# Perceiver block on one core: the end of the kernel with batch 1's attention sum in TensorE's bank and roundings on ScalarE

## The chip, the cores and the metric

The kernel runs on 1 core of one Trainium2 chip. The metric is the device time of one execution in microseconds, as the median of several runs. Engines are TensorE (PE in the profile, its weight loads PEld), VectorE (DVE), ScalarE (ACT), GpSimd (POOL) and SyncE (SP, which issues the DMAs).

## The reference

Two sequences of 256 tokens of 256 features pass through three parts, each added to the running input: a decoder of four layers with cross attention, one windowed attention, and a feed forward part with quantised weights and activations. The change lies in the last two.

```python
x = x + _L0_xattn_ref(_layernorm(x), ctx, ...)
x = x + _L0_attn_ref(_layernorm(x), ...)      # y = xn + msg @ wo.T; layernorm(y) * gamma + beta
x = x + _L0_ffn_ref(_layernorm(x), ...)
def _act_quant(x):
    scale = 127.0 / jnp.clip(jnp.max(jnp.abs(x), axis=-1, keepdims=True), 1e-05)
    xq = jnp.clip(jnp.round(x * scale), -128.0, 127.0) / scale
gate = jax.nn.silu(_bitlinear(x, w_gate)); up = _bitlinear(x, w_up)
return _bitlinear(gate * up, w_down)          # weights -1, 0, 1 times a scale; inner size 1024
```

## The kernel before

The 512 tokens are four tiles of 128 (t = 0 to 3), two for each batch b. `X0` holds the running input, `hs` (rows of the tile `HE`) the normalised tokens, `X` (rows of `XE`) a scratch tile and the outputs. Four fp32 banks `psD` of 512 columns take TensorE's results in turn (`next_bank`); four more, the tile `QD`, take the gate and up products in two pairs `QB[j]`, one for each half j of the 1,024 inner features.

Each engine runs its own list of steps, written out by hand near the end of its block (TensorE L1185 to 1229, ScalarE up to L1823, VectorE L2530 to 2582, GpSimd up to L2809). Steps meet through semaphores alone, so the order of each list decides what queues behind what. On VectorE `done` adds to a semaphore and waits for it, so that a step that reads its predecessor's result starts after it.

The end, for batch 1, goes so. TensorE multiplies the attention's messages `oT` with the output weight (`out_proj`, L539 to 548). VectorE adds the normalised tokens (`window_sum`), takes mean and variance (`layernorm_stats`; GpSimd forms the power -0.5, `ln_rsqrt`), applies gamma (`window_gamma`), adds to `X0` (`window_residual`), and takes mean and variance again. `layernorm_apply(7, 1)` normalises, `round_tokens` finds each token's largest magnitude, scales, and rounds by adding and subtracting the number MAGIC (12582912), which leaves whole numbers in bf16. TensorE transposes these (`rounded_T`, L787) and VectorE copies the transposed tile back (L2141).

Then for each tile t: TensorE forms gate and up products in halves (`quantised_gate_up`, L797); ScalarE applies silu (`quantised_gates`, L1485); VectorE multiplies gate and up (`quantised_hidden`, L2146), finds the maximum and scale of the 1,024 products (`hidden_scales`, four instructions in `quantise_scales` and L2157); ScalarE scales and adds MAGIC (`scale_hidden`, L1490); VectorE subtracts it (`round_hidden`, L2159); TensorE transposes (`hidden_T`, L809); VectorE copies back (`hidden_T`, L2163); TensorE multiplies with the down weight (`quantised_down`, L818); VectorE scales and adds to `X0` (`output`, L2168); SyncE stores the tile (L1307). The down weight is made ternary by ScalarE in two pieces (`ternary(2)`, `ternary(3)`, L1475), and the first down product waits for both:

```python
pe.wait_ge(tern_set, 4)
pe.wait_ge(*emptied(NL, f"gT{t}"))
```

A gate product of tile t waits until VectorE has read the same pair of banks for tile t - 1 (`quad_free(qu_free, 2 * t + j + 1, ...)`).

## Time and profile before

| | |
|---|---|
| median of 3 runs | 574.45 us (574.3 to 574.61) |
| the profiled execution | 574.83 us |
| its span in the profile | 573.09 us (573.1 on the page) |
| granted TensorE clock, mean | 0.997 of full speed |
| TensorE, VectorE, ScalarE, GpSimd busy | 521.0, 349.2, 283.2, 113.4 us |
| end of the last VectorE instruction | 569.96 us |

The span runs from the first to the last recorded instruction or transfer; the execution's own time has 1.74 us around it. Busy shares are averages over the whole span. To see one stage, a view is cut to a stretch of time: which engine has no gaps, and what the others wait for. In a row of the order of time, the first number is the start, the second the time from the first start to the last end of the merged instructions, and the bracket gives the idle time before and what ended it.

### The profile page before, as it was taken

To read this page: it belongs to the slowest core of one execution; us is meant where nothing else is said; L and a number is where in the kernel's file an instruction comes from. 1 tells how busy PE (TensorE), PEld (TensorE's weight loads), DVE (VectorE), ACT (ScalarE), POOL (GpSimd) and SP (SyncE) were. 2 spreads that over 40 slices of the span, in tenths; PEclk is the share of its full clock that TensorE was granted. 3 is DMA by queue.
4 is the path that set the end of the run, shared out by engine and by line. 5 is a ranking of instruction groups with operands and counts; after the bars stand their busy time and mean duration, and the time that the engine had idled before them with its cause. 6 is when DMAs were issued, how large, how long until landed. Compare 5 with 4: busy or idle time off the path is not lost.

```text
span 573.1 us, 15284 instructions
## 1 busy us (share of the span) xinstructions
PE 521.0 (91%) x6586; PEld 405.8 (71%) x6586; DVE 349.2 (61%) x669; ACT 283.2 (49%) x509; POOL 113.4 (20%) x126
## 2 busy tenths in 40 slices
PE   5888898999998999999998989999989989999764
PEld 3566665988777767988676659988667669987523
...
GB/s 303 182 2 2 3 314 18 11 65 1 196 65 3 13 63 3 74 0 1 222 2 39 75 2 1 75 1 101 122 8 24 76 1 2 1 0 2 2 2 42
DMA packets 5515, 30.40 MB, mean 53 GB/s; under 512 B 1217, under 2 KB 2113, under 8 KB 3778
## 3 DMA queue, kind: packets, MB, share of 16 engines
...
## 4 chain that ended last, share of the span: by engine, by line
PE 76%; DVE 13%; ACT 8%; issue 2%; DMA 0%; POOL 0%; DVEq 0%
PE psD L350 16%; PE QD L694 14%; PE psD L707 10%; PE QD L446 7%; PE QD L486 5%; DVE AQ L1918 4%; ACT PTR L1353 4%; PE psD L344 3%; PE psD L506 3%; PE QD L479 3%; PE psD L694 2%; PE psD L527 2%; PE psD L513 2%; PE psD L387 2%; DVE MX L1915 2%
## 5 line engine op out<-in xcount | busy, mean ns | idle before, releaser
L1353 ACT ACTIVATE PTR<-QD 128x2048 f32<-128x2048 f32 x40 | 75.2, 1880 | 52.8 <-PE QD L486 46.1
L1918 DVE TENSOR_REDUCE AQ<-QD 128x8 f32<-128x2048 f32 (+1 forms) x24 | 55.0, 2292 | 29.4 <-PE QD L446 29.3
L694 PE MATMUL QD<-HH,WFH 128*128 128x256 f32 x224 | 69.0, 308 | 0.0
L2607 POOL TENSOR_TENSOR rstd<-ms,mhalf 128x2 f32<-128x2 f32 x26 | 18.3, 705 | 232.6 <-ACT HE L1319 231.5
L694 PE MATMUL QD<-HL,WFH 128*128 128x256 f32 x224 | 63.3, 282 | 0.0
L694 PE MATMUL QD<-HH,WFL 128*128 128x256 f32 x224 | 63.2, 282 | 0.0
L1915 DVE TENSOR_REDUCE MX<-QD 128x16 f32<-128x2048 f32 x16 | 36.7, 2294 | 39.6 <-PE QD L446 39.6
L707 PE MATMUL psD<-WC,HID 128*128 128x256 f32 x256 | 58.5, 381 | 0.0
L2023 DVE TENSOR_TENSOR WFL<-WC,WFH 128x512 fp32r<-128x512 f32 x64 | 44.4, 701 | 18.6 <-ACT WFH L1399 18.1
L350 PE MATMUL psD<-WAB,hT 128*128 128x256 f32 (+1 forms) x152 | 52.8, 485 | 1.0 <-DVE hT L1856 1.0
L2654 POOL TENSOR_SCALAR_AFFINE_SELECT PTR<-PTR 128x1024 f32<-128x1024 f32 (+1 forms) x24 | 34.5, 1440 | 93.0 <-ACT PTR L1353 93.0
L707 PEld LDWEIGHTS psD<-WC,HID 128*128 128x128 f32 x256 | 47.5, 190 | 7.3 <-issue 1.0
L1399 ACT ACTIVATE WFH<-WC 128x512 fp32r<-128x512 f32 x64 | 40.2, 630 | 24.7 <-PE QD L694 24.1
L446 PE MATMUL QD<-AQ 32*128 32x128 f32 (+1 forms) x1024 | 46.5, 312 | 0.0
L694 PEld LDWEIGHTS QD<-HH,WFH 128*128 128x128 f32 x224 | 42.7, 191 | 3.0 <-issue 2.7
L694 PEld LDWEIGHTS QD<-HH,WFL 128*128 128x128 f32 x224 | 42.8, 191 | 1.7 <-issue 1.4
L694 PEld LDWEIGHTS QD<-HL,WFH 128*128 128x128 f32 x224 | 42.7, 191 | 0.0
L446 PEld LDWEIGHTS QD<-AQ 32*128 32x128 f32 x1024 | 35.1, 185 | 7.7 <-issue 5.5
L1319 ACT ACTIVATE HE<-XE 128x257 f32<-128x257 f32 x48 | 19.7, 413 | 38.3 <-DVE XE L1960 38.3
L350 PEld LDWEIGHTS psD<-WAB,hT 128*128 128x128 f32 x152 | 27.7, 194 | 14.7 <-issue 10.6
L350 PE MATMUL psD<-WAB,oT 128*128 128x256 f32 x144 | 35.3, 388 | 3.0 <-ACT oT L1365 3.0
L1361 ACT ACTIVATE QO<-psD 128x512 f32<-128x512 f32 (+1 forms) x40 | 20.5, 513 | 34.3 <-PE psD L513 18.1
...
## 6 DMA issues: line engine op xcount, KB each, us to landing
...
```

What stands on the lines that cost most here:

```text
L350: mm = pe.matmul(bank(l, use)[:, col:col + n], lhs(k), rhs(k), start=(k == 0), stop=(k == KT - 1))
L446: mm = pe.matmul(quad[a][:, at:at + keys], QKT[b][rows(a), s, q * P:(q + 1) * P], QKT[b][rows(a), s, L:L + keys], start=False, stop=True, ...
L486: mm = pe.matmul(quad[a][:, at:at + P], QKT[b][rows(a), s, L + k * P:L + (k + 1) * P], Q2[rows(a), n * P:(n + 1) * P], start=(at == 0), st ...
L694: mm = pe.matmul(S[:, w * L:(w + 1) * L], wp[:, m, :], hp[:, k, :], start=(k == 0 and j == 0), stop=(k == KT - 1 and j == 2))
L707: mm = pe.matmul(bank(l, use)[:, t * D:(t + 1) * D], AT[b][:, f, t * P:(t + 1) * P], Wd[:, f, :], start=(f == 0 and t == 0), stop=(f == FT ...
L1353: nc.scalar.activation(PTR[:, r % 2, :], QD[:, :], ACT.Exp, scale=SCALE if r < SELF_ROUNDS else 1.0).then_inc(t_exp, 1)
L1361: nc.scalar.activation(OA[:, 0:n], bank(l, use)[:, 0:n], ACT.Copy).then_inc(free(l, use), 1)
L1399: nc.scalar.activation(w_high(n), WCt[:, :, f * P:(f + 1) * P], ACT.Copy).then_inc(wh_set, 1)
L1915: v = dve.tensor_reduce(MX[:, :, ss[0] // 2, :].rearrange("p t (r c) -> p r c t", r=SG_H)[:, :, at:at + 2, :], QD[:, :].rearrange("p (r s ...
L1918: v = dve.tensor_reduce(QKR[b][:, t, 0, h, MAXROW].rearrange("p (s r) -> p r s", r=SG_H), QD[:, :].rearrange("p (r s n) -> p r s n", r=4, ...
L2023: dve.tensor_tensor(w_low(n), WCt[:, :, f * P:(f + 1) * P], w_high(n), ALU.subtract).then_inc(wl_set, 1)
L2654: nc.gpsimd.affine_select(T, T, [[0, 16 // (t + 1)], [1, P]], ALU.is_ge, 0.0, base=0, channel_multiplier=-1)\
```

## The change

It has four parts, all in the end of the kernel.

- The sum of batch 1's attention: TensorE first multiplies the normalised tokens with the identity into the bank `mwo1`, then adds the projection to it (`out_proj_on_tokens`). VectorE's addition goes; statistics and gamma read the bank (`window_sum_stats`, `window_sum_gamma`).
- Batch 1's tokens: ScalarE subtracts them from their mean (`centre`), VectorE takes the maximum of that and forms one factor out of the two scales, with its sign turned (`centred_scales`), ScalarE scales and rounds (`scale_tokens`, `unbias_tokens`). The gates and up products no longer wait for a second scale product (`token_sgu` makes both at once).
- The gated tiles 0 to 2 are rounded on ScalarE (`unbias_hidden`). The upper limit of 127 moves into the copies of the transposed tiles. The maximum, clamp and reciprocal become three steps that stand apart in VectorE's list, and the scale for the output is formed by GpSimd (`hidden_sgu`).
- The last gated tile is scaled half on VectorE, half on ScalarE, then rounded on VectorE, transposed and copied in halves of 512.

The diff, with indentation cut, without declarations of semaphores and without the lists of ScalarE and VectorE, whose result the rows below it show:

```diff
+def out_proj_on_tokens(b, source):
+    use = f"mwo{b}"
+    next_bank(NL, use)
+    pe.wait_ge(an_set[b], 1)
+    pe.wait_ge(*free_for(NL, use))
+    for t in range(QT):
+        pe.matmul(bank(NL, use)[:, t * D:(t + 1) * D], ident, hs[:, 2 * b + t, :], start=(t == 0), stop=False,
+                  skip_group_check=True)
+    pe.wait_ge(*emptied(NL, source))
+    for t in range(QT):
+        for k in range(KT):
+            mm = pe.matmul(bank(NL, use)[:, t * D:(t + 1) * D], oT[b][:, k, t * P:(t + 1) * P], Wt[:, 3, k, :],
+                           start=False, stop=(k == KT - 1), skip_group_check=True)
+    mm.then_inc(full(NL, use), 1)
...
+def last_hidden_T(half):
+    use = f"gT{LAST}{half}"
+    next_bank(NL, use)
+    pe.wait_ge(last_set, half + 1)
+    pe.wait_ge(*free_for(NL, use))
+    for n in range(FT // 2):
+        at = half * F // 2 + n * P
+        mm = pe.transpose(bank(NL, use)[:, :].bitcast(BF16)[:, n * P:(n + 1) * P], GQ(LAST)[:, at:at + P], identB[:, :])
+    mm.then_inc(full(NL, use), 1)
 def quantised_down(t):
     next_bank(NL, f"d{t}")
     pe.wait_ge(tern_set, 4)
-    pe.wait_ge(*emptied(NL, f"gT{t}"))
     pe.wait_ge(*free_for(NL, f"d{t}"))
+    if t < LAST:
+        pe.wait_ge(*emptied(NL, f"gT{t}"))
     for f in range(FT):
+        if t == LAST and f % (FT // 2) == 0:
+            pe.wait_ge(*emptied(NL, f"gT{LAST}{f // (FT // 2)}"))
         mm = pe.matmul(bank(NL, f"d{t}")[:, 0:D], GQT(t)[:, f * P:(f + 1) * P],
                        WQ[2][:, f * D:(f + 1) * D], start=(f == 0), stop=(f == FT - 1))
     mm.then_inc(full(NL, f"d{t}"), 1)
     window_pv(1, 1)
-    out_proj(NL, 1, "mwo1", Wt[:, 3, :, :], "pw1")
+    out_proj_on_tokens(1, "pw1")
     rounded_T(0)
     quantised_gate_up(0, 0)
     quantised_gate_up(0, 1)
     rounded_T(1)
     quantised_gate_up(2, 0)
     quantised_gate_up(2, 1)
+    hidden_T(0)
     quantised_gate_up(3, 0)
     quantised_gate_up(3, 1)
-    hidden_T(0)
     hidden_T(1)
     quantised_down(0)
     hidden_T(2)
+    last_hidden_T(0)
+    last_hidden_T(1)
     quantised_down(1)
-    hidden_T(3)
     quantised_down(2)
     quantised_down(3)
...
 def quantised_gates(t, j):
-    act.wait_ge(sgu_set, t // 2 * 2 + 2)
+    act.wait_ge(sgu_set, t // 2 + 1)
     act.wait_ge(qg_full, 2 * t + j + 1)
...
+def scale_last_hidden():
+    act.wait_ge(gq_scale_set, LAST + 1)
+    nc.scalar.activation(GU(LAST)[:, F // 2:F], GU(LAST)[:, F // 2:F], ACT.Copy, scale=am2[:, LAST, 2:3], bias=MAGIC)\
+      .then_inc(last_scaled, 1)
+def centre(b):
+    act.wait_ge(ln_var[b], 4)
+    for t in range(QT):
+        a = nc.scalar.activation(hs[:, 2 * b + t, :], X0[:, 2 * b + t, :], ACT.Identity, scale=-1.0,
+                                 bias=mv[:, 6 + b, t, 0:1])
+    a.then_inc(cen_set, 1)
+def scale_tokens(b):
+    act.wait_ge(tok_scale_set, 1)
+    for t in range(QT):
+        a = nc.scalar.activation(hs[:, 2 * b + t, :], hs[:, 2 * b + t, :], ACT.Copy, scale=am[:, 2 * b + t, 1:2], bias=MAGIC)
+    a.then_inc(tok_scaled, 1)
+def unbias_tokens(b):
+    act.wait_ge(tok_scaled, 1)
+    for t in (2 * b, 2 * b + 1):
+        nc.scalar.activation(xq[:, t, :], hs[:, t, :], ACT.Copy, bias=-MAGIC).then_inc(xq_set[b], 1)
+def unbias_hidden(t):
+    act.wait_ge(gq_scaled, t + 1)
+    nc.scalar.activation(GQ(t), GU(t), ACT.Copy, bias=-MAGIC).then_inc(gq_set, 1)
...
+def window_sum_stats(b):
+    use, n = f"mwo{b}", 4 + b
+    dve.wait_ge(*filled(NL, use))
+    for t in range(QT):
+        v = dve.bn_stats(bst[:, n, t, :], bank(NL, use)[:, t * D:(t + 1) * D])
+    done(v)
+    for t in range(QT):
+        v = dve.bn_aggr(mv[:, n, t, :], bst[:, n, t, :])
+    done(v)
+    dve.tensor_scalar(lve[:, n, :], mv[:, n, :, 1], LN_EPS, None, ALU.add).then_inc(ln_var[b], 1)
+def window_sum_gamma(b):
+    use = f"mwo{b}"
+    for t in range(QT):
+        v = dve.scalar_tensor_tensor(hs[:, 2 * b + t, :], bank(NL, use)[:, t * D:(t + 1) * D], mv[:, 4 + b, t, 0:1],
+                                     vec[:, D:2 * D], ALU.subtract, ALU.mult)
+    v.then_inc(free(NL, use), 1)
+    dve.wait_ge(*emptied(NL, use))
...
-    for w in range(2):
-        dve.tensor_scalar(sgu[:, 2 * b:2 * b + 2, w], am[:, 2 * b:2 * b + 2, 3], mw[:, w:w + 1], None, ALU.mult)\
-           .then_inc(sgu_set, 1)
+    token_sgu(b)
+def token_sgu(b):
+    dve.tensor_tensor(sgu[:, 2 * b:2 * b + 2, 0:2], am[:, 2 * b:2 * b + 2, 3].unsqueeze(2).broadcast_to([P, 2, 2]),
+                      mw[:, 0:2].unsqueeze(1).broadcast_to([P, 2, 2]), ALU.mult).then_inc(sgu_set, 1)
+def centred_scales(b):
+    ts = slice(2 * b, 2 * b + 2)
+    dve.wait_ge(cen_set, 1)
+    done(dve.tensor_reduce(am[:, ts, 0], hs[:, ts, :], AX_X, ALU.max, apply_absolute_value=True))
+    dve.wait_ge(ln_rstd[b], 4)
+    done(dve.tensor_tensor(am[:, ts, 0], am[:, ts, 0], lrs[:, 6 + b, :], ALU.mult))
+    done(dve.tensor_scalar(am[:, ts, 3], am[:, ts, 0], 1e-5, 1.0 / 127.0, ALU.max, ALU.mult))
+    done(dve.reciprocal(am[:, ts, 2], am[:, ts, 3]))
+    dve.scalar_tensor_tensor(am[:, ts, 1], am[:, ts, 2], -1.0, lrs[:, 6 + b, :], ALU.mult, ALU.mult).then_inc(tok_scale_set, 1)
+    token_sgu(b)
 def rounded_T(b):
     dve.wait_ge(*filled(NL, f"fn{b}"))
     dve.tensor_scalar(xqT[b][:, :, :].rearrange("p k n -> p (k n)"), bank(NL, f"fn{b}")[:, :].bitcast(BF16)[:, 0:KT * L],
-                      -128.0, None, ALU.max).then_inc(free(NL, f"fn{b}"), 1)
+                      -128.0, 127.0, ALU.max, ALU.min).then_inc(free(NL, f"fn{b}"), 1)
 def quantised_hidden(t, j):
-    dve.wait_ge(sgu_set, t // 2 * 2 + 2)
+    dve.wait_ge(sgu_set, t // 2 + 1)
     dve.wait_ge(qu_full, 2 * t + j + 1)
     dve.wait_ge(qg_free, 2 * t + j + 1)
     dve.scalar_tensor_tensor(GU(t)[:, j * 512:(j + 1) * 512], QB[j][1],
                              sgu[:, t, 1:2], GR(t)[:, j * 512:(j + 1) * 512], ALU.mult, ALU.mult)\
        .then_inc(qu_free, 1)
-def hidden_scales(t):
+def hidden_max(t):
     dve.wait_ge(qu_free, 2 * t + 2)
-    quantise_scales(t, 1, GU(t).unsqueeze(1), 1)
-    dve.tensor_scalar(sgu[:, t, 2:3], am2[:, t, 3:4], mw[:, 2:3], None, ALU.mult).then_inc(gq_scale_set, 1)
-def round_hidden(t):
-    dve.wait_ge(gq_scaled, t + 1)
-    dve.tensor_scalar(GQ(t), GU(t), MAGIC, 127.0, ALU.subtract, ALU.min).then_inc(gq_set, 1)
+    dve.tensor_reduce(am2[:, t:t + 1, 0], GU(t).unsqueeze(1), AX_X, ALU.max, apply_absolute_value=True).then_inc(gq_max_set, 1)
+def hidden_clamp(t):
+    dve.wait_ge(gq_max_set, t + 1)
+    dve.tensor_scalar(am2[:, t:t + 1, 3], am2[:, t:t + 1, 0], 1e-5, 1.0 / 127.0, ALU.max, ALU.mult).then_inc(gq_step_set, 1)
+def hidden_inverse(t):
+    dve.wait_ge(gq_step_set, t + 1)
+    dve.reciprocal(am2[:, t:t + 1, 2], am2[:, t:t + 1, 3]).then_inc(gq_scale_set, 1)
 def hidden_T(t):
     dve.wait_ge(*filled(NL, f"gT{t}"))
-    dve.tensor_scalar(GQT(t), bank(NL, f"gT{t}")[:, :].bitcast(BF16), -128.0, None, ALU.max)\
+    dve.tensor_scalar(GQT(t), bank(NL, f"gT{t}")[:, :].bitcast(BF16), -128.0, 127.0, ALU.max, ALU.min)\
        .then_inc(free(NL, f"gT{t}"), 1)
+def scale_last_hidden():
+    dve.wait_ge(gq_scale_set, LAST + 1)
+    done(dve.tensor_scalar(GU(LAST)[:, 0:F // 2], GU(LAST)[:, 0:F // 2], am2[:, LAST, 2:3], MAGIC, ALU.mult, ALU.add))
+def round_last_hidden(half):
+    if half:
+        dve.wait_ge(last_scaled, 1)
+    at = slice(half * F // 2, (half + 1) * F // 2)
+    dve.tensor_scalar(GQ(LAST)[:, at], GU(LAST)[:, at], MAGIC, 127.0, ALU.subtract, ALU.min).then_inc(last_set, 1)
+def last_hidden_T(half):
+    use = f"gT{LAST}{half}"
+    dve.wait_ge(*filled(NL, use))
+    at = slice(half * F // 2, (half + 1) * F // 2)
+    dve.tensor_scalar(GQT(LAST)[:, at], bank(NL, use)[:, :].bitcast(BF16)[:, 0:F // 2], -128.0, None, ALU.max)\
+       .then_inc(free(NL, use), 1)
 def output(t):
-    dve.wait_ge(gq_scale_set, t + 1)
+    dve.wait_ge(hidden_sgu_set, t + 1)
     dve.wait_ge(*filled(NL, f"d{t}"))
     dve.scalar_tensor_tensor(X[:, t, :], bank(NL, f"d{t}")[:, 0:D], sgu[:, t, 2:3], X0[:, t, :],
                              ALU.mult, ALU.add).then_inc(free(NL, f"d{t}"), 1)
     layernorm_stats(6, 0, X0)
     layernorm_apply(6, 0, X0, hs, done)
     round_tokens(0)
-    window_sum(1)
-    layernorm_stats(5, 1, X)
+    window_sum_stats(1)
     rounded_T(0)
-    window_gamma(1)
+    window_sum_gamma(1)
     window_residual(1)
     layernorm_stats(7, 1, X0)
...
+def hidden_sgu(t):
+    pool.wait_ge(gq_scale_set, t + 1)
+    nc.gpsimd.tensor_tensor(sgu[:, t, 2:3], am2[:, t, 3:4], mw[:, 2:3], ALU.mult)\
+        .then_inc(hidden_sgu_set, 1)
```

GpSimd's list ends with `hidden_sgu(0)` to `hidden_sgu(3)`.

ScalarE from the first gates to its end. Before (`AQ<-QD,sgu` is a gate step, `AQ<-AQ,am` a scaling, `WC<-WF,negmagic` the ternary weight):

```order
L1488 ACTIVATE AQ<-QD,sgu 128x512 [waits qg_full,sgu_set] x7
L1492 ACTIVATE AQ<-AQ,am 128x1024 [waits gq_scale_set]
L1482 ACTIVATE WC<-WF,negmagic 128x1024 [waits tern_step]
L1492 ACTIVATE AQ<-AQ,am 128x1024 [waits gq_scale_set]
L1488 ACTIVATE AQ<-QD,sgu 128x512 [waits qg_full,sgu_set]
L1492 ACTIVATE AQ<-AQ,am 128x1024 [waits gq_scale_set] x2
```

ScalarE in the changed kernel, from the gates of tile 1's second half (`HID<-AQ` is the rounding of a gated tile):

```order
L1523 ACTIVATE AQ<-QD,sgu 128x512 [waits qg_full,sgu_set]
L1527 ACTIVATE AQ<-AQ,am 128x1024 [waits gq_scale_set]
L1554 ACTIVATE HID<-AQ 128x1024 [waits gq_scaled]
L1523 ACTIVATE AQ<-QD,sgu 128x512 [waits qg_full,sgu_set] x2
L1527 ACTIVATE AQ<-AQ,am 128x1024 [waits gq_scale_set]
L1554 ACTIVATE HID<-AQ 128x1024 [waits gq_scaled]
L1523 ACTIVATE AQ<-QD,sgu 128x512 [waits qg_full,sgu_set] x2
L1517 ACTIVATE WC<-WF,negmagic 128x1024 [waits tern_step]
L1527 ACTIVATE AQ<-AQ,am 128x1024 [waits gq_scale_set]
L1554 ACTIVATE HID<-AQ 128x1024 [waits gq_scaled]
L1531 ACTIVATE AQ<-AQ,am 128x512 [waits gq_scale_set]
```

The gates of tiles 2 and 3 now stand behind scaling and rounding of tiles 0 and 1, and the ternary weight behind the last gates.

VectorE between the two first gated products and tile 2's. Before (`HE` are the tokens, `QO` their rounded copy and its transpose, `am<-AQ` a maximum):

```order
L2150 SCALAR_TENSOR_TENSOR AQ<-QD,sgu,AQ 128x512 [waits qg_free,qu_full,sgu_set] x2
L2056 TENSOR_SCALAR HE<-X,mv,lrs 128x256 [waits ln_rstd1]
L2056 TENSOR_SCALAR HE<-X,mv,lrs 128x256
L2076 TENSOR_REDUCE am<-HE 128x2 [waits v_step]
L2077 TENSOR_SCALAR am<-am 128x2 [waits v_step]
L2078 RECIPROCAL am<-am 128x2 [waits v_step]
L2133 TENSOR_SCALAR HE<-HE,am 128x256 [waits v_step]
L2133 TENSOR_SCALAR HE<-HE,am 128x256
L2136 TENSOR_SCALAR QO<-HE 128x256 [waits v_step]
L2136 TENSOR_SCALAR QO<-HE 128x256
L2138 TENSOR_SCALAR sgu<-am,mw 128x2 x2
L2150 SCALAR_TENSOR_TENSOR AQ<-QD,sgu,AQ 128x512 [waits qg_free,qu_full,sgu_set] x2
```

VectorE in the changed kernel, the same place:

```order
L2251 SCALAR_TENSOR_TENSOR AQ<-QD,sgu,AQ 128x512 [waits qg_free,qu_full,sgu_set] x2
L2234 TENSOR_REDUCE am<-HE 128x2 [waits cen_set]
L2236 TENSOR_TENSOR am<-am,lrs 128x2 [waits ln_rstd1,v_step]
L2237 TENSOR_SCALAR am<-am 128x2 [waits v_step]
L2238 RECIPROCAL am<-am 128x2 [waits v_step]
L2239 SCALAR_TENSOR_TENSOR am<-am,lrs 128x2 [waits v_step]
L2227 TENSOR_TENSOR sgu<-am,mw 128x2x2
L2257 TENSOR_REDUCE am<-AQ 128x1 [waits qu_free]
L2251 SCALAR_TENSOR_TENSOR AQ<-QD,sgu,AQ 128x512 [waits qg_free,qu_full,sgu_set]
L2261 TENSOR_SCALAR am<-am 128x1 [waits gq_max_set]
L2244 TENSOR_SCALAR QO<-psD 128x512 [waits d_full3]
L2265 RECIPROCAL am<-am 128x1 [waits gq_step_set]
```

Six token steps of 256 are gone from the list, and tile 0's maximum stands before the gated products of tile 1.

## Rows read from the trace of the kernel before

**Rows 1.** The page, part 1: busy time, share, instructions.
```profile
PE 521.0 (91%) x6586; PEld 405.8 (71%) x6586; DVE 349.2 (61%) x669; ACT 283.2 (49%) x509; POOL 113.4 (20%) x126
```
**Rows 2.** Busy time by stretch; the last columns are granted clock, DMA share, GB/s.
```profile
505.00:541.27 36.27, 34.00 (x472) 27.59 (x470) 15.69 (x47) 19.93 (x26) 9.65 (x9) 1.00 0.01 2
541.27:569.96 28.69, 16.17 (x104) 8.22 (x101) 27.20 (x64) 10.70 (x13) 1.38 (x2) 0.94 0.04 11
```
**Rows 3.** Order of time, around the projection of batch 1.
```profile
536.43 2.10 PE L781 MATMUL psD<-PTR,AQ 128*32 128x128 f32 x96 [0.85 <-issue]
...
539.24 1.99 PE L350 MATMUL psD<-WAB,oT 128*128 128x256 f32 x8 [0.71 <-ACT oT L1365]
...
541.27 0.69 DVE L2111 TENSOR_TENSOR XE<-HE,psD 128x512 f32<-128x512 f32 x1 [0.28 <-PE psD L350]
542.00 0.75 DVE L2046 BATCH_NORM_STATS2 bst<-XE 128x6 f32<-128x256 f32 x2
```
**Rows 4.** Order of time, the tokens of batch 1.
```profile
546.48 1.41 DVE L2150 SCALAR_TENSOR_TENSOR AQ<-QD,sgu,AQ 128x512 f32<-128x512 f32 x2
546.62 0.69 POOL L2612 TENSOR_TENSOR lrs<-lve,mhalf 128x2 f32<-128x2 f32 x1 [2.61 <-DVE lve L2051]
...
547.80 0.73 DVE L2056 TENSOR_SCALAR HE<-X,mv,lrs 128x256 f32<-128x256 f32 x2
...
548.57 0.69 DVE L2076 TENSOR_REDUCE am<-HE 128x2 f32<-128x512 f32 x1
...
550.90 0.40 PE L794 MATMUL psD<-identB,QO 128*128 128x128 bf16 x4 [1.64 <-DVE QO L2136]
551.02 1.41 DVE L2150 SCALAR_TENSOR_TENSOR AQ<-QD,sgu,AQ 128x512 f32<-128x512 f32 x2
```
**Rows 5.** Order of time, tile 2's products and the last maximum.
```profile
552.86 4.44 PE L806 MATMUL QD<-WAB,QO 128*128 128x512 bf16 x12 [1.56 <-DVE QO L2143]
...
554.50 0.75 DVE L2150 SCALAR_TENSOR_TENSOR AQ<-QD,sgu,AQ 128x512 f32<-128x512 f32 x1
...
562.74 1.21 DVE L2076 TENSOR_REDUCE am<-AQ 128x1 f32<-128x1024 f32 x1
```
**Rows 6.** VectorE's groups by form from 541.27 us: busy us, mean ns.
```profile
L2165 DVE TENSOR_SCALAR HID<-psD 128x1024 bf16<-128x1024 bf16 x4 | 2.7, 685 | 0.1
L2161 DVE TENSOR_SCALAR HID<-AQ 128x1024 bf16<-128x1024 f32 x4 | 2.6, 684 | 0.0
L2171 DVE SCALAR_TENSOR_TENSOR XE<-psD,sgu,X 128x256 f32<-128x256 f32 x4 | 1.9, 480 | 0.4 <-PE psD L825 0.4
...
L2117 DVE SCALAR_TENSOR_TENSOR HE<-XE,mv,bias 128x256 f32<-128x256 f32 x2 | 0.9, 476 | 0.0
```
**Rows 7.** ScalarE's groups by form from 500 us.
```profile
L1488 ACT ACTIVATE AQ<-QD,sgu 128x512 f32<-128x512 f32 x8 | 5.5, 686 | 12.1 <-PE QD L806 12.1
L1492 ACT ACTIVATE AQ<-AQ,am 128x1024 f32<-128x1024 f32 x4 | 4.6, 1142 | 2.2 <-DVE sgu L2157 2.2
...
L1482 ACT ACTIVATE WC<-WF,negmagic 128x1024 bf16<-128x1024 f32 x2 | 2.3, 1143 | 0.0
...
L1458 ACT ACTIVATE AQ<-psD 128x256 f32<-128x256 f32 x4 | 1.3, 383 | 0.1
```
**Rows 8.** Order of time on ScalarE, where it has no gaps.
```profile
557.55 1.14 ACT L1492 ACTIVATE AQ<-AQ,am 128x1024 f32<-128x1024 f32 x1
558.59 1.14 ACT L1482 ACTIVATE WC<-WF,negmagic 128x1024 bf16<-128x1024 f32 x1
```
**Rows 9.** Order of time, the end.
```profile
567.47 1.91 PE L825 MATMUL psD<-WC,HID 128*128 128x256 bf16 x16
...
569.48 0.48 DVE L2171 SCALAR_TENSOR_TENSOR XE<-psD,sgu,X 128x256 f32<-128x256 f32 x1 [0.39 <-PE psD L825]
```
**Rows 10.** Busy time by stretch, columns as in rows 2.
```profile
549.30:552.86 3.56, 0.40 (x5) 0.26 (x5) 3.46 (x12) 0.32 (x1) 0.00 (x0) 1.00 0.01 5
553.40:556.70 3.30, 3.30 (x9) 1.17 (x8) 3.13 (x8) 1.38 (x2) 0.00 (x0) 0.51 0.00 0
```

51 lines of the change are left out of this document (35 added, 16 removed).

## The prediction

> **What bounds the kernel now.** I read the page first. TensorE is busy for 91% of the span and VectorE for 61% [rows 1]. That is an average over stages, and all that this change touches lies in the last 32 us. So the second view was the busy time by stretch [rows 2]: up to 541.27 us TensorE is busy for 34.00 of 36.27 us; from there to the end of the last VectorE instruction at 569.96, VectorE is busy for 27.20 of 28.69 us, TensorE for 16.17 and ScalarE for 10.70. The tail is a VectorE queue with two helpers that mostly wait for it. Taking work off VectorE there shortens the run, until ScalarE or TensorE ends last in its place. The third view, the order of time, gives the points against which I lay the new schedule [rows 3 to 5]; the grouped instructions give the prices [rows 6, 7], and [rows 8, 9] show ScalarE at its densest and the end.
>
> **The change part by part.** I follow the new VectorE order from 538.5 us and note its lead over the old one.
>
> *The sum in TensorE's bank.* The residual tile is added by two identity matmuls of 128x256 in fp32. Four such matmuls (eight passes) take 1.99 us [rows 3], so two take 1.0. Their input is ready long before; they stand in TensorE's queue after the product that ends at 536.43 + 2.10 = 538.53, so they end at 539.53. The projection could start at 539.24, when ScalarE's copy was there [rows 3]; it now starts 0.29 later and ends at 541.52. Before, VectorE began the addition at 541.27 and the statistics at 542.00; now the statistics start at about 541.55: lead 0.45. Bounds: 0.73 if the identity pair hides wholly, -0.27 if it adds its full 1.0 behind the copy. I take 0.45, since both ends of TensorE's gap stand in the rows. The statistics and the gamma step now read the bank; a fused step of 256 elements takes 480 ns from a bank and 476 from memory [rows 6], so that costs nothing. The two scale products in one instruction save 0.13 in front of a wait, so nothing.
>
> *Batch 1's tokens.* The first gated product moves from 546.48 to 546.03, and after two of them VectorE is free for the next step at 547.35 (before 547.80 [rows 4]). Meanwhile ScalarE takes the mean off: two 256-element steps at 0.38 each [rows 7], done by 546.9, so hidden. VectorE then goes straight to the reduction (0.72 with its wait) where before two normalising steps took 547.80 to 548.57. Then come one small product more (0.2), the clamp and reciprocal (0.4), and two small products (0.25) in place of scaling, rounding and two products, which took until 551.02. VectorE is free at 548.95: lead 2.05. Scaling and rounding of the tokens go to ScalarE: four steps of 256, 1.45 us from 549.05 to 550.5. TensorE's transposes start at 550.6 (before 550.90), and their copy on VectorE can end by 551.45, which lets the gate and up products of tile 2 start at 551.55 instead of 552.86 [rows 4, 5]. VectorE fills the wait with the first maximum (1.21) and a gated product.
>
> *Where the lead goes: ScalarE.* From 551.6 ScalarE has, for tile 0, scaling and rounding of 1,024 elements. Scaling takes 1.142 us, and the nearest row for an output in bf16 is 1.143 [rows 7]. The second waits for the first: 551.6 to 553.95. Only then does it reach the gates of tile 2 (0.69 each), so VectorE's product on tile 2 starts at about 554.6, where it stood at 554.50 [rows 5]. The lead of 2 us is gone at this point; VectorE has done its maxima instead. It goes on on ScalarE: gates until 555.1, tile 1 to 557.3, both gates of tile 3 to 558.5, the ternary half of the down weight to 559.55, tile 2 to 561.95. VectorE, behind the gates, multiplies tile 3 at 558.0 and 558.75, so that its last maximum starts at 559.55, where it stood at 562.74 [rows 5]: lead 3.2, because three gated products and three maxima no longer queue behind the roundings. ScalarE ends last in almost every wait here. An unseen cost is what a ScalarE step waits on its own predecessor's result; between 0.04, what VectorE takes for its own result (541.27 + 0.69 to 542.00 [rows 3]), and 0.10, what it takes for TensorE's last product (567.47 + 1.91 to 569.48 [rows 9]), I take 0.04, since both are one engine's own; four such pairs stand on the path, so the other end adds 0.24. No reason excludes more; that is rival C.
>
> The row on ScalarE's side says 1.142 against VectorE's 0.684 for the same 1,024 elements [rows 6, 7]. The Trainium skill, "ScalarE: Activation LUTs", Rules for kernel authors, says to use VectorE and not ScalarE for add, multiply and maximum; the trace agrees on the price. By the rule alone this change would be a loss of 0.46 for each rounding moved; by the rows of the stretch it pays as long as ScalarE has the room, and that room is used up. The same page, What ACT_TABLE_LOAD costs, prices a step with constant scale and bias at 186 ns + 0.833 ns an element, 1.04 for the roundings; by it the sum would come out 0.3 lower.
>
> *The last tile.* The last maximum ends at 560.75. The copies of transposed tiles 0 and 1 (0.685 each, a little overlapped; their second comparison is priced at nothing, since a rounding with two operations takes 0.684 for as many elements [rows 6]) fill VectorE to 561.95 with the small steps between. Then half of the last tile's scaling (0.42) runs on VectorE at 562.15 beside the other half on ScalarE (0.69, to 562.9), then the rounding in halves (0.35 each) with the first output between, the second half ending at 563.8. TensorE transposes the second half to 564.2. From here TensorE is the bound: three down products, each eight matmuls. Sixteen took 1.91 [rows 9], so 24 take 2.87: 567.1, and the last output starts at 567.25 and ends at 567.73, where it ended at 569.48 + 0.48 = 569.96. **Lead at the end 2.25 us.** First-tile products wait for the last ternary piece (559.55) and VectorE's copy (561.35); both are early enough for 561.4.
>
> *Other queues.* GpSimd gets four tiny products. Its step here took 0.69 for two columns [rows 4]; the last of the four would be done by 563.1, output wants it at 567.2, so they cost nothing until they are 4 us late. SyncE's four stores keep their order; the last store ran 3.13 us past the last VectorE instruction to the end of the span, and I leave that. Rows up to 538 do not move.
>
> **The sum.** The profiled execution took 574.83 us for a span of 573.09, and 574.83 - 2.25 = 572.6. The median of the runs shown is 574.45, 0.38 less than the profiled one, so the same gain would put the median at 572.2. The profiled one had a stretch of half speed (next part), which the median may not have had in full. Since the new order is more open to such a stretch, I stay at **572.6**. A difference under 0.2% (1.15 us) can't be told from none here.
>
> **The rivals.**
> *Half speed at the down products (B).* Between 549.30 and 552.86 TensorE was busy for 0.40 us; then the granted clock was 0.51 from 553.4 to 556.7, the lower level of 1.2 GHz, and nine matmuls took the whole 3.30 us [rows 10]. The new order has a quiet time at a worse place: after the transposes of tile 1 end at 558.1, nothing is ready until 561.4. A stretch like the one in the rows holds 1.65 us of work at full speed and costs at most as much again; behind 561.4 part of it falls in waits, so I put the loss at 0.7 to 1.2 us. The median would be 572.2 + 1.0 = 573.2. For it: a similar quiet time did it here. Against: TensorE has gate products and transposes up to 558.1, more work just before than there was then, and the three runs before lie within 0.31 us, so such a stretch costs the old order little either way. The rule of "TensorE: Matmul & The Clock Gate" in the Trainium skill, its Part 1, says that low speed is the default and activity lifts it; by that rule, the trace agrees.
> *ScalarE eats it (C).* ScalarE has eight steps in a row from 551.6 to the last gates at 558.5, and the last maximum hangs on the eighth. If each costs 0.22 more than its row, through waits on its own results or on memory that VectorE writes, 1.8 of the 2.25 are gone: 574.0, no change. For it: no row shows such a chain of steps that wait for each other. Against: independent steps of 1.14 followed each other at 1.04 there [rows 8].
> *ScalarE too long, slower than before (D).* One mechanism: VectorE's gated products of tiles 2 and 3 stand behind ScalarE's roundings. Place: 551.6 to 558.5. From 572.2 to the 0.2% bound at 575.6 are 3.4 us, so it decides from 0.43 us more for each of the eight; at 0.5 each the time is 576.2. The rule of use above is this rival's rule, and the trace agrees with its price, not with its result. Against: the prices of 1.142 and 1.143 come from this stage itself.
> *The change doesn't do what it says.* If the first matmuls hold the projection back by a whole 1.0, 0.7 of the lead at 541.5 go, but ScalarE's chain starts at the tokens and shifts with it: 572.9. It is inside the range.
>
> **How the numbers follow.** As summed (A): 0.60. B: 0.20; it lies at the 0.2% bound, 0.12 on the faster side. C: 0.13. D: 0.07. Faster 0.72, same 0.21, slower 0.07. The range goes from 571.8 (A at 572.2, the cheaper roundings and a shorter start) to 574.2, which takes in B and most of C.
>
> **What would show it.** Right: statistics from the bank near 541.5; VectorE's token reduction near 547.4 without wait; ScalarE nearly without gaps from 551.6 to 562; VectorE waiting for ScalarE before tile 2's and tile 3's products; the last maximum near 559.6; the last 24 matmuls back to back; the last output waiting for TensorE. Wrong: gaps in ScalarE's row behind its own results, roundings well over 1.14, a low granted clock after 560, or VectorE still busy without waits to the end, which would mean that it lost less work than I count.

## The result, and the profile after

The changed kernel takes a median of 574.03 us (20 runs, 573.64 to 575.51); the kernel before, in the runs beside it, 574.81 (20 runs, 574.30 to 577.36). The ratio over all runs is 0.9979, with a 95% interval of 0.9971 to 0.9988, which stands for 1.2 us; the two medians are 0.8 us apart. The prediction had set a bound of 0.2% for a difference, and the interval lies on both sides of it. The profiled execution took 573.64 us for a span of 570.93. The span fell by 2.16 us against the one before (573.09), where 2.25 had been forecast, and the time by only 1.19; what failed lies outside the span. The next fences show the inside of it. One run of the kernel before, among the twelve called aa_before below, took 1,735 us; it counts in the median of the time there, and is left out of spans and ranges.

The page, part 1, answers [rows 1]: VectorE lost 4.8 us of busy time, ScalarE gained 4.7.

```profile
PE 520.9 (91%) x6590; PEld 407.1 (71%) x6590; DVE 344.4 (60%) x658; ACT 287.9 (50%) x518; POOL 113.9 (20%) x130
```

Busy time by stretch of the changed kernel, columns as in [rows 2]: up to the start of the statistics, and from there to the end of the last VectorE instruction.

```profile
505.00:541.54 36.54, 34.98 (x477) 28.53 (x476) 15.50 (x46) 19.90 (x26) 9.89 (x9) 1.00 0.01 2
541.54:567.77 26.23, 15.15 (x105) 8.84 (x102) 22.75 (x54) 15.74 (x22) 2.14 (x6) 0.93 0.04 13
```

The tail, the second stretch, is 26.2 us long instead of 28.7, and VectorE works in 22.8 of them instead of 27.2. It now waits for 3.5 us where it waited for 1.5: the bound has moved. The order of time shows to whom.

Order of time of the changed kernel: start, length, engine, line, what it does, and in brackets the wait before it. First the projection with the identity pairs (L555) and the token statistics; it answers [rows 3] and [rows 4].

```profile
538.73 1.13 PE L555 MATMUL psD<-HE,const 128*128 128x256 f32 x4
538.85 0.60 ACT L1400 ACTIVATE oT<-psD 128x512 f32<-128x512 f32 x1 [1.22 <-PE psD L801]
539.70 1.89 PE L560 MATMUL psD<-WAB,oT 128*128 128x256 f32 x8
541.62 0.76 DVE L2193 BATCH_NORM_STATS2 bst<-psD 128x6 f32<-128x256 f32 x2 [0.56 <-PE psD L560]
...
546.11 1.41 DVE L2251 SCALAR_TENSOR_TENSOR AQ<-QD,sgu,AQ 128x512 f32<-128x512 f32 x2
546.20 0.91 ACT L1537 ACTIVATE HE<-X,mv 128x256 f32<-128x256 f32 x2 [0.66 <-DVE lve L2119]
547.43 0.68 DVE L2234 TENSOR_REDUCE am<-HE 128x2 f32<-128x512 f32 x1
548.90 1.21 DVE L2257 TENSOR_REDUCE am<-AQ 128x1 f32<-128x1024 f32 x1
550.66 0.40 PE L814 MATMUL psD<-identB,QO 128*128 128x128 bf16 x4 [1.77 <-ACT QO L1550]
```

Then the middle, where ScalarE goes from tile 0's scaling to the gates of tile 3 almost without a gap, and VectorE waits for it twice; it answers [rows 5] and [rows 8].

```profile
551.62 1.15 ACT L1527 ACTIVATE AQ<-AQ,am 128x1024 f32<-128x1024 f32 x1 [0.44 <-DVE am L2265]
552.81 1.06 ACT L1554 ACTIVATE HID<-AQ 128x1024 bf16<-128x1024 f32 x1
553.77 1.25 ACT L1523 ACTIVATE AQ<-QD,sgu 128x512 f32<-128x512 f32 x2
554.57 1.41 DVE L2251 SCALAR_TENSOR_TENSOR AQ<-QD,sgu,AQ 128x512 f32<-128x512 f32 x2 [0.69 <-ACT AQ L1523]
...
557.85 0.75 DVE L2251 SCALAR_TENSOR_TENSOR AQ<-QD,sgu,AQ 128x512 f32<-128x512 f32 x1 [0.62 <-ACT AQ L1523]
559.35 1.22 DVE L2257 TENSOR_REDUCE am<-AQ 128x1 f32<-128x1024 f32 x1
```

ScalarE's new steps by form, from 541 us (busy us, mean ns), beside [rows 7]:

```profile
L1527 ACT ACTIVATE AQ<-AQ,am 128x1024 f32<-128x1024 f32 x3 | 3.4, 1148 | 0.5 <-DVE am L2265 0.4
L1554 ACT ACTIVATE HID<-AQ 128x1024 bf16<-128x1024 f32 x3 | 3.2, 1057 | 0.1
...
L1537 ACT ACTIVATE HE<-X,mv 128x256 f32<-128x256 f32 x2 | 0.9, 500 | 0.7 <-DVE lve L2119 0.7
```

And the end, which answers [rows 9], with a window on the granted clock, which answers [rows 10]:

```profile
561.32 1.86 PE L859 MATMUL psD<-WC,HID 128*128 128x256 bf16 x8 [3.50 <-DVE HID L2269]
561.98 0.19 POOL L2800 TENSOR_TENSOR sgu<-am,mw 128x1 f32<-128x1 f32 x1 [2.32 <-DVE am L2265]
564.40 2.78 PE L859 MATMUL psD<-WC,HID 128*128 128x256 bf16 x24
567.29 0.48 DVE L2292 SCALAR_TENSOR_TENSOR XE<-psD,sgu,X 128x256 f32<-128x256 f32 x1 [0.39 <-PE psD L859]
```

```profile
560.60:563.98 3.38, 2.66 (x18) 2.17 (x19) 2.93 (x8) 1.78 (x2) 0.19 (x1) 0.50 0.01 5
```

The last output ends at 567.29 + 0.48 = 567.77, where it ended at 569.96. Eight down products took 1.86 at 561.32, at a granted clock of 0.50.

Two sizes have to be read apart from here on, run by run: the **span**, from the first to the last recorded instruction, and what a run takes **outside** it, the time less the span. In the kernel before, the second is 1.74 for the profiled execution (574.83 less 573.09), and 1.68 to 1.78 in every run beside the experiments. In the changed kernel it is 2.71 for the profiled execution, and 1.81 to 3.56 over its 20 runs, with a median of 2.74.

### The profile page after: what moved, and what is told of

It is laid out like the page before. It is cut to its first block, busy times and chain, and to the rows that moved or that the text cites. A ratio compares the mean times of both kernels' runs of the same rounds, so it can differ in the third digit from the quotient of the medians.

```text
span 570.9 us, 15296 instructions
## 1 busy us (share of the span) xinstructions
PE 520.9 (91%) x6590; PEld 407.1 (71%) x6590; DVE 344.4 (60%) x658; ACT 287.9 (50%) x518; POOL 113.9 (20%) x130
## 4 chain that ended last, share of the span: by engine, by line
PE 78%; DVE 10%; ACT 8%; issue 2%; DMA 0%; POOL 0%; DVEq 0%; ACTq 0%
PE psD L354 16%; PE QD L714 14%; PE psD L727 10%; PE QD L450 7%; PE QD L490 5%; DVE AQ L1986 4%; ACT PTR L1388 4%; PE psD L348 3%; PE psD L510 3%; PE QD L483 3%; PE psD L714 2%; PE psD L531 2%; PE psD L517 2%; PE psD L391 2%; DVE MX L1983 2%
## 5 line engine op out<-in xcount | busy, mean ns | idle before, releaser
L2761 POOL TENSOR_TENSOR HID<-HID,const 128x256 f32<-128x256 f32 (+1 forms) x32 | 27.7, 887 | 42.6 <-DVE HID L1933 42.6
```

The source lines that it names most:

```text
L2761: g = nc.gpsimd.tensor_tensor(r[:, 0:m, to:to + half], q[:, 0:m, of:of + half], sin[:, t, to:to + half].unsqueeze(1).broadcast_to([P, m, h ...
```

## The experiments

Each kernel ran 11 or 12 times (a_fill, a_vecround and a_best_fill six times), beside runs of the kernel before on the same chip (23, 34 and 29 runs for the three groups). Ratios are to those; spans and the time outside are medians, in us. The kernel before had medians of 575.91, 575.54 and 574.90 there, with median spans of 574.2, 573.8 and 573.2, so only the ratio compares across groups.

| kernel | ratio (95%) | median | span | outside |
|---|---|---|---|---|
| group 1: aa_before | 0.9997 (0.9983 to 1.0011) | 575.03 | 573.3 | 1.73 |
| a_fill | 0.9935 (0.9921 to 0.9949) | 571.95 | 570.2 | 1.73 |
| a_nosum | 0.9966 (0.9954 to 0.9979) | 573.95 | 572.3 | 1.75 |
| a_vecround | 0.9958 (0.9944 to 0.9972) | 573.14 | 570.8 | 2.43 |
| group 2: aa_after | 0.9979 (0.9967 to 0.9992) | 574.24 | 571.2 | 3.00 |
| a_pad2 | 0.9967 (0.9952 to 0.9981) | 572.97 | 571.3 | 1.72 |
| a_pad16 | 0.9959 (0.9943 to 0.9976) | 573.03 | 571.3 | 1.75 |
| b_fill | 1.0004 (0.9991 to 1.0017) | 576.02 | 574.3 | 1.70 |
| group 3: b_fill2 | 1.0001 (0.9989 to 1.0014) | 575.16 | 573.4 | 1.80 |
| a_vec0 | 0.9975 (0.9964 to 0.9987) | 573.89 | 571.0 | 2.72 |
| a_best | 0.9977 (0.9966 to 0.9989) | 574.00 | 570.1 | 3.82 |
| a_best_fill | 0.9953 (0.9938 to 0.9969) | 572.51 | 570.7 | 1.77 |

**The kernel before, unchanged.**

> The kernel before, unchanged, so that its spans and clocks are seen run by run. The question: the profiled span fell by 2.2 us (573.1 to 570.9), the median time only by 0.8 (574.81 to 574.03). Theory 1, half-speed stretches: all runs of the kernel before have a mean granted clock of 0.997 (one such stretch in the tail) and spans within 0.5 us of 573.1, where 12 of 20 runs of the change showed 0.994 and spans 0.3 to 2.8 us over 570.9. Theory 2, time outside the span: the old kernel's time lies 1.7 us over its span in every run, the new one's 2.2 to 3.0. Theory 3, chance: the profiled span of before was a long one; most of its spans are near 572 and its time lies 2.5 over them as the changed kernel's does. Ratio to before 1.000.

The other runs took 574.43 to 577.34 us, for spans of 572.7 to 575.6 and 1.68 to 1.77 outside. The granted clock of the whole run was 0.987 to 0.997, where I had taken 0.997 for all. The profiled one had half speed from 544.48 to 547.90 and from 558.14 to 564.96 us; the window is the second, and the rows lie in it. In the first profile of the same program the only low stretch was that of [rows 10].

```profile
558.14:564.96 6.82, 5.58 (x28) 3.02 (x28) 6.61 (x14) 3.98 (x5) 0.00 (x0) 0.50 0.01 2
```

```profile
558.12 1.86 PE L806 MATMUL QD<-WAB,QO 128*128 128x512 bf16 x4 [1.39 <-DVE AQ L2150]
561.04 1.89 PE L815 MATMUL psD<-identB,HID 128*128 128x128 bf16 x16 [1.07 <-DVE HID L2161]
562.95 1.86 PE L825 MATMUL psD<-WC,HID 128*128 128x256 bf16 x8
```

So where a stretch falls differs from run to run of one program, and the old order has them too. Its spans spread over 3 us, but not in step with the mean clock: at 0.988 there is a span of 572.8 and one of 575.6. What a stretch costs would then depend on where it falls, which single traces can't show for all runs. The part outside hardly moves.

**The change with TensorE kept busy.** Products that nobody reads fill its quiet times ahead of the token transposes and of the first down product; they go to the half of the bank that the step behind them leaves unused, and the wait on the ternary weight moves behind them.

```diff
 # transposes of the tokens, batch 1
+                pe.wait_ge(*free_for(NL, use))
+                if b == 1:
+                    for _ in range(12):
+                        pe.matmul(bank(NL, use)[:, D:2 * D], identB[:, :], WQ[0][:, 0:D], start=True, stop=True)
                 pe.wait_ge(xq_set[b], 2)
-                pe.wait_ge(*free_for(NL, use))
...
 # down product
-                pe.wait_ge(tern_set, 4)
                 pe.wait_ge(*free_for(NL, f"d{t}"))
+                if t == 0:
+                    for _ in range(24):
+                        pe.matmul(bank(NL, "d0")[:, D:2 * D], identB[:, :], WQ[0][:, 0:D], start=True, stop=True)
+                pe.wait_ge(tern_set, 4)
```

> The changed kernel with matmuls that nobody reads in TensorE's two quiet times of the tail: 12 before the token transposes (about 549 to 550.3), 24 before the first down product (about 558 to 560.6). Theory 1: the granted clock stays at its upper level in the tail in all runs, mean clock 0.998 or more, all spans near 570.7, and the median time falls by 0.3 to 0.6 us against the change, to about 573.5. Rival: the stretches cost nothing (they fall where TensorE has slack), and times and spans stay as they are, 574.0, or get worse by the added matmuls, 574.3.

Six runs of 571.90 to 572.08, spans of 570.2 and 570.3, clock 1.00 in all of them: the spread is gone, and this is the fastest kernel measured. The order of time (L858 is the fill), and the same window of time as above for the change:

```profile
557.74 2.78 PE L858 MATMUL psD<-WAB,identB 128*128 128x256 bf16 x24
561.40 1.03 PE L865 MATMUL psD<-WC,HID 128*128 128x256 bf16 x8 [0.88 <-DVE HID L2275]
564.01 2.78 PE L865 MATMUL psD<-WC,HID 128*128 128x256 bf16 x24
566.90 0.48 DVE L2298 SCALAR_TENSOR_TENSOR XE<-psD,sgu,X 128x256 f32<-128x256 f32 x1 [0.39 <-PE psD L865]
```

```profile
560.60:563.98 3.38, 2.08 (x24) 1.68 (x25) 3.31 (x10) 1.84 (x3) 0.19 (x1) 1.00 0.01 5
```

Eight down products take 1.03 here and 1.86 in the change; the last output starts at 566.90, although the first down product started 0.08 later. In the span the fill is worth 0.5 us against the change's shortest runs (570.7) and 1.1 against the median of its 20 (571.35). The median time fell by 2.1, and the other 1.0 of that lies outside, where 2.74 went back to 1.73. That I had not foreseen, and group 2 is about it.

**Without the sum in the bank.** The projection, the addition and the statistics are the old ones.

```diff
-                out_proj_on_tokens(1, "pw1")
+                out_proj(NL, 1, "mwo1", Wt[:, 3, :, :], "pw1")
-                window_sum_stats(1)
+                window_sum(1)
+                layernorm_stats(5, 1, X)
-                window_sum_gamma(1)
+                window_gamma(1)
```

> The changed kernel with the attention sum of batch 1 back on VectorE (no identity matmuls, an addition of 512 columns, statistics from memory). By the order of time the sum in the bank gave 0.37 to 0.45 us at 541.5: theory A, all later waits shift with it, span 571.3, time 574.4 (0.4 slower than the change). Rival: ScalarE's chain from 551.6 on absorbs it, span 570.9, time as the change.

The addition is back, and the statistics stand 0.72 behind it (ScalarE's copy ahead of the projection starts at 539.51 in this run and at 538.85 in the change's, so all of its tail lies some 0.7 later):

```profile
540.16 1.99 PE L354 MATMUL psD<-WAB,oT 128*128 128x256 f32 x8 [0.71 <-ACT oT L1400]
...
542.20 0.69 DVE L2179 TENSOR_TENSOR XE<-HE,psD 128x512 f32<-128x512 f32 x1 [0.48 <-PE psD L354]
542.92 0.76 DVE L2114 BATCH_NORM_STATS2 bst<-XE 128x6 f32<-128x256 f32 x2
```

Shortest spans are 571.2 against 570.7, medians 572.3 against 571.35: the sum in the bank is worth 0.5 to 0.9, where I took 0.45. The two profiles say 0.64: the statistics start 1.30 later (542.92 for 541.62), of which the copy accounts for 0.66. The part outside is 1.75, so the time is no longer than the change's: another case in which span and time tell different things.

**Three roundings back on VectorE.** The gated tiles 0, 1 and 2 are rounded by VectorE, ahead of the products of tiles 2 and 3 and of the last tile's scaling; ScalarE keeps the scaling.

```diff
-                unbias_hidden(0)
...
+            def round_hidden(t):
+                dve.wait_ge(gq_scaled, t + 1)
+                dve.tensor_scalar(GQ(t), GU(t), MAGIC, 127.0, ALU.subtract, ALU.min).then_inc(gq_set, 1)
```

> The changed kernel with the three roundings of gated tiles back on VectorE (tile 0 after the second reciprocal, tile 1 after the third maximum, tile 2 after the last reciprocal), all else as in the change. ScalarE loses 3 x 1.06 us, VectorE gains 3 x 0.6. Theory that ScalarE is the bound of the middle: VectorE's waits of 0.69 at 554 and 0.62 at 557 shrink and pay for the roundings, so the end moves by 0 to +0.3 us: span 571.0, time 574.1. Rival, that moving the roundings is what gives the gain: the end moves by the whole 1.8 us, span 572.7, time 575.3.

```profile
553.88 0.67 DVE L2266 TENSOR_SCALAR HID<-AQ 128x1024 bf16<-128x1024 f32 x1
554.47 1.41 DVE L2248 SCALAR_TENSOR_TENSOR AQ<-QD,sgu,AQ 128x512 f32<-128x512 f32 x2
...
559.14 1.22 DVE L2254 TENSOR_REDUCE am<-AQ 128x1 f32<-128x1024 f32 x1
```

VectorE does the rounding in the time in which it had waited for ScalarE: the product on tile 2 starts at 554.47 (554.57 in the change), the last maximum at 559.14 (559.35). The median span of six runs is 570.8 against 571.35, where I had expected the end to move by 0 to 0.3 us later. As far as six runs show (570.0 to 571.5), moving these roundings to ScalarE gave nothing, then; in the middle ScalarE is the bound, as the prediction had it, and the change has handed it more than it had room for.

**The change again, and with two small products.** The first is the change unchanged. The others have 2 and 16 unread products of 32 columns ahead of the first down product, which TensorE does in a quiet time.

```diff
-                pe.wait_ge(tern_set, 4)
                 pe.wait_ge(*free_for(NL, f"d{t}"))
+                if t == 0:
+                    for _ in range(2):
+                        pe.matmul(bank(NL, "d0")[:, D:D + 32], identB[:, :], WQ[0][:, 0:32], start=True, stop=True)
+                pe.wait_ge(tern_set, 4)
```

> The changed kernel, unchanged. In 20 runs its time lay 1.8 to 3.6 us over its span (median 2.7), where the kernel before, the one with filled quiet times and the one without the sum in the bank all lay 1.73 over theirs. Theory P, the program's layout: it comes back here, median time 574.0, 2.7 over the span. Rival: a matter of those runs alone; here 1.73 over the span and a median of 573.2. Mean clocks 0.997 and 0.994, as before.

> The changed kernel with 2 matmuls of 32 columns that nobody reads before the first down product, in a quiet time: 4 more instructions in TensorE's program, no time in the tail. Theory P (layout of TensorE's program decides the time outside the span): the kernel with the sum off has 8 instructions fewer there and shows 1.73, so a shift by a few instructions can remove it; time over span 1.73, median 573.1. Rival: time over span stays near 2.7, median 574.0.

> As the last, with 16 such matmuls (32 instructions, about 0.5 us in the quiet time, little of it array work). Theory P: time over span 1.73, median 573.1, clocks still 0.997 and 0.994 from run to run. Rival, that what helped in the filled kernel was the clock alone: time over span near 2.7.

Span and time less span, in rising order of span:

```
aa_after  570.8 3.25 | 571.0 3.03 | 571.0 3.03 | 571.0 3.24 | 571.1 2.67 | 571.1 2.70
          571.2 3.03 | 571.2 3.30 | 571.6 2.73 | 571.8 2.98 | 571.9 2.42 | 573.3 1.92
a_pad2    570.6 1.77 | 570.6 1.77 | 570.9 1.69 | 570.9 1.72 | 571.0 1.79 | 571.2 1.73
          571.3 1.70 | 571.8 1.72 | 571.9 1.71 | 573.1 1.70 | 573.1 1.75 | 573.5 1.72
```

The medians of the span agree within 0.1 us; the part outside is 3.00 in one kernel and 1.72 in the other, and no run of the one reaches into the range of the other. The medians of the time differ by 1.27 us, all of it outside. So the change costs 1.0 to 1.3 us more outside the span than the kernel before, and two products that compute nothing take it away. It follows the program, not its work. What in the program decides is open: the recorded first and last instructions, the stores, and the loading of instructions look alike in kernels of 1.7 and of 3 us. Where it sits the traces do show: behind the last recorded instruction. The record of TensorE's granted clock runs on behind the span, and in all fourteen traces it ends 0.31 to 0.32 us later than the time outside would put it: 2.05 behind the span in the kernel before (1.74 outside), 2.06 in a_pad2 (1.74), 3.03 in the change (2.71), 3.58 in aa_after (3.26), 3.85 in a_best (3.53). Time ahead of the first instruction would not have moved that end. In the change and in a_best, though not in a_vec0, the longest span comes with the least outside (573.3 with 1.92, 573.7 with 1.81 in the first 20 runs, 571.1 with 3.54 in a_best), as if the end waited for something that is not recorded; what that is, is not shown.

**The old order with TensorE kept busy.** First 8 and 12 unread products ahead of the token transposes of the batches and 18 ahead of the first gated transposes; then 12 more ahead of tile 2's gate products.

```diff
 # b_fill
+                pe.wait_ge(*free_for(NL, use))
+                for _ in range(12 if b else 8):
+                    pe.matmul(bank(NL, use)[:, D:2 * D], identB[:, :], WQ[0][:, 0:D], start=True, stop=True)
                 pe.wait_ge(xq_set[b], 2)
-                pe.wait_ge(*free_for(NL, use))
...
+                pe.wait_ge(*free_for(NL, f"gT{t}"))
+                if t == 0:
+                    for _ in range(18):
+                        pe.matmul(bank(NL, "gT0")[:, 0:D], identB[:, :], WQ[0][:, 0:D], start=True, stop=True)
                 pe.wait_ge(gq_set, t + 1)
-                pe.wait_ge(*free_for(NL, f"gT{t}"))
...
 # b_fill2 has besides, ahead of the gate products
+                if (t, j) == (2, 0):
+                    n = len(uses)
+                    pe.wait_ge(d_free[n % DBANKS], n // DBANKS + 1)
+                    for _ in range(12):
+                        pe.matmul(psD[n % DBANKS][:, 0:D], identB[:, :], WQ[0][:, 0:D], start=True, stop=True)
```

> The kernel before with its quiet times filled by matmuls that nobody reads: 8 before the first token transposes, 12 before the second, 18 before the first transposes of a gated tile. It shows what the old order is worth without half speed. Theory 1: mean clock 0.999 or 1.0 in all runs, spans within 0.2 us of each other at 572.5 to 572.8, time 574.3, against 571.95 for the changed kernel filled in the same way: the change itself is then worth 2.3 us, as its order of time says. Rival: the old order loses nothing to the stretches; median as before, near 575, since its long runs come from elsewhere.

> The kernel before with all four quiet times filled: as the last filled one, and 12 more unread matmuls before tile 2's gate products, where that one still had its half-speed stretch (553.6 to 557.0). Theory 1: mean clock 1.0 in all runs, spans within 0.2 us of each other at 572.5, time 574.2; the changed kernel filled has 570.2 and 571.95, so the change is worth 2.3 us by itself. Rival: spans still spread from 572.8 to 575 as with three quiet times filled, so the long runs of the old order do not come from the clock.

b_fill kept one stretch, at tile 2's products in the profiled run; five of its spans were 572.8 to 573.3, seven 574.3 to 575.0, with a clock of 0.997 in the long ones and 0.997 or 0.998 in the short ones, so the mean clock does not tell them apart. b_fill2 had a clock of 0.999 to 1.00 in eight runs, with spans of 572.8 to 573.5, and in four a single stretch (0.997), with 574.1 to 574.8. Neither beats the kernel before by its ratio. The profiled run of b_fill2 is one of the four; its stretch fell on the last products:

```profile
566.34 1.91 PE L835 MATMUL psD<-WC,HID 128*128 128x256 bf16 x8
568.04 1.06 PE L825 MATMUL psD<-identB,HID 128*128 128x128 bf16 x8
...
569.14 0.69 DVE L2175 TENSOR_SCALAR HID<-psD 128x1024 bf16<-128x1024 bf16 x1 [1.33 <-PE psD L825]
...
571.20 0.48 DVE L2181 SCALAR_TENSOR_TENSOR XE<-psD,sgu,X 128x256 f32<-128x256 f32 x1 [0.39 <-PE psD L835]
```

VectorE waits 1.33 for transposes that stand behind eight down products, both at half speed. A stretch costs about 1.4 us here, by the medians of the four spans (574.55) and of the eight (573.15). At full clock the old order has 572.8 at the shortest and 573.15 in the middle, the new one 570.2, so in the span the change is worth 2.6 to 2.9 us. The fills are not the same in the two, and those of the old order may cost something themselves: its shortest span without fills is 572.5, which leaves 2.3.

**One rounding back, and a new order.** a_vec0 returns the rounding of tile 0 alone to VectorE (with a semaphore of its own), just ahead of tile 2's product. a_best takes that, lets the gates and products of tile 3 go ahead on ScalarE and TensorE, and the second down product ahead of the last transposes:

```diff
 # ScalarE
-                unbias_hidden(1)
                 quantised_gates(3, 0)
                 quantised_gates(3, 1)
+                unbias_hidden(1)
 # TensorE
-                hidden_T(0)
                 quantised_gate_up(3, 0)
                 quantised_gate_up(3, 1)
+                hidden_T(0)
...
+                quantised_down(1)
                 last_hidden_T(0)
                 last_hidden_T(1)
-                quantised_down(1)
```

> The changed kernel with the rounding of tile 0 alone back on VectorE, in its 0.69 us of waiting before tile 2's first gated product. If ScalarE is the bound between 551.6 and 558.5, one step of 1.06 less there brings tile 2's gates 0.5 to 1.0 earlier and the end 0.9 earlier: shortest span 569.9, most runs 0.3 to 1.0 under the change's span of 571.2. Rival: VectorE's own work fills the gap, span as the change's or with all three roundings back on VectorE, 570.8.

> As the last, and tile 1's rounding on ScalarE behind tile 3's gates, TensorE's transposes of tile 0 behind tile 3's products, and its second down product ahead of the last transposes. By the prices of the changed kernel's rows the last output ends 1.2 us earlier than in the change, span 569.5 in runs with one half-speed stretch or none and 570.3 with two; time 1.73 over it, or 2.7 if the layout falls badly: 571.3 or 572.3. Rival: a wait of TensorE's queue takes the place (transposes of tile 0 behind tile 3's products), span 570.7.

The shortest spans came as expected: 569.8 in a_vec0 and 569.4 in a_best, against 570.7 in the change. The median of a_best is 570.1, the lowest of all; that of a_vec0 is 571.0, 0.2 under the change's and less of a gain than expected. The time did not: a_best has 3.54 to 4.12 outside and ends at 574.00. The rows of its profile show a stretch again, on tile 1's down product and on the last transposes, for which VectorE waits 1.35.

```profile
562.59 1.92 PE L860 MATMUL psD<-WC,HID 128*128 128x256 bf16 x8
...
564.96 0.75 DVE L2290 TENSOR_SCALAR HID<-psD 128x512 bf16<-128x512 bf16 x2 [1.35 <-PE psD L847]
```

**The new order with both fills of a_fill.**

> As the last, with TensorE's quiet times filled as in the filled changed kernel. Theory 1: all runs at mean clock 1.0, spans within 0.2 us at 569.1, time 570.8, the shortest of all. Rival: the 24 unread matmuls, 2.6 us, now reach into the time of the first transposes and cost up to 1 us: span 570.2, time 571.9.

The part outside is 1.77 again, with a clock of 0.998 to 1.00, but the span is 570.7 where a_fill has 570.2. The rival of that expectation came true: in the new order the fill starts later and reaches over the time at which the first down product could start.

```profile
559.42 2.78 PE L859 MATMUL psD<-WAB,identB 128*128 128x256 bf16 x24
562.04 1.04 PE L866 MATMUL psD<-WC,HID 128*128 128x256 bf16 x8
...
563.18 0.48 DVE L2302 SCALAR_TENSOR_TENSOR XE<-psD,sgu,X 128x256 f32<-128x256 f32 x1 [0.73 <-PE psD L866]
```

The first output waits 0.73 for it. A shorter fill there, and a_vec0 or a_best with two padding products, were not tried; by the shortest spans of a_best and a_vec0 and 1.73 outside, the best runs of the latter would stand at 571.1 and 571.5, which is an estimate.

## Why the prediction was right, and where not

**What bounds the kernel, and the schedule: right.** VectorE's queue was the bound of the tail, and work taken off it shortened the run until ScalarE ended last. The dates of the prediction against the trace: statistics 541.55 and 541.62, token reduction 547.35 and 547.43, tile 2's product 554.6 and 554.57, tile 3's 558.0 and 557.85, the last maximum 559.55 and 559.35, the first down product 561.4 and 561.32, the last output 567.25 and 567.29. The lead at the end was to be 2.25 and is 2.19. That the last date fits so well is in part luck: by the last maximum the run was 0.2 ahead of the forecast, and a stretch of half speed that the sum leaves out took this back. Without it, in a_fill, the last output starts at 566.90. Of the change's four parts the runs separate only two, the sum in the bank and the roundings; the tokens on ScalarE, the last tile in halves and the new order of the lists were not run one by one, so their share of the 2.2 us is read from the rows and not shown.

**Single prices.** *The sum in the bank:* 0.45 taken; the statistics start at 541.62 for 542.00 before, although this run's tail stood some 0.2 later, and a_nosum gives 0.5 to 0.9. *The mean by ScalarE:* 0.38 each taken from [rows 7], 0.50 measured; the mean is an operand from memory there, not a constant, and it stayed hidden. The Trainium skill, "ScalarE: Activation LUTs", What ACT_TABLE_LOAD costs, prices such a step at 280 ns + 0.833 ns an element, an estimate of 0.49 for 256; the trace agrees with 0.50. *The roundings:* 1.143 taken, 1.057 measured. The estimate of 1.04 that the prediction worked out from the same section of the Trainium skill was the nearer. *GpSimd's products:* 0.69 taken, 0.19 measured, hidden either way. *A step behind its own engine's result* waits about 0.04 on ScalarE (551.62 + 1.15 to 552.81), as taken, so rival C fell, and with it D; the measured 574.03 is the time that C gave, 574.0, but not for C's reason. That three gated products and maxima no longer queue behind roundings was right, but a_vecround shows that this came from the order, not from the move to ScalarE.

**The step that failed: "The sum."** It took the whole gain off the profiled time, 574.83 - 2.25, and so carried the time around the span, 1.74, over from the old kernel unchanged, having named only the 3.13 us between the last VectorE instruction and the end of the span. The latter stayed (567.77 to 570.93 is 3.16), the former did not: 2.71 in the profiled execution. 570.93 + 1.74 would have been 572.67, for a forecast of 572.6; with 2.71 it is 573.64. Nothing in the trace of before could give this term; it should have had a width in the range, which its steady 1.7 in one program does not provide, since the next program has its own.

**Rival B, half speed at the down products: partly true, and at its price.** The stretch fell exactly there, at 560.6 to 563.98, but two things were different from the prediction. It is not a single case that comes or stays away: 7 of the change's 20 runs have a clock of 0.997 and 13 have 0.994. A stretch of 3.41 us at half speed, as this one (560.57 to 563.98), takes 0.003 off the mean of 571 us, so every run has one or two. And the old order has as many or more, 0.987 to 0.997. The price is 0.5 to 1.1 by a_fill, where I put 0.7 to 1.2; in the profiled run the first eight down products took 0.83 longer than in a_fill (1.86 for 1.03), and the last output started 0.39 later (567.29 for 566.90). The Trainium skill, "TensorE: Matmul & The Clock Gate", Part 1, has low speed as the default and activity as what lifts it; a_fill agrees, with a clock of 1.00 once the quiet times were filled.

**The time** was forecast as 572.6, and the median is 574.03. Of the 1.4 between, 1.0 is outside the span (2.74 for 1.74), and 0.5 is in it: 571.35 as the median span, where 572.6 less 1.74 is 570.9. I took the three runs shown, within 0.31 of each other, for the whole spread of the old kernel; its spans reach from 572.5 to 575.6. Sign and range held. The gain was about half of what was forecast; most of the rest was given back by a term that lies behind the last recorded instruction.

**Doing what it says:** the identity matmuls took 1.13 and held the projection back by 0.25 (ScalarE's copy is there at 538.85 + 0.60 = 539.45, the projection starts at 539.70), not by 1.0.
